# Local attention's scores as three fp32r products of query and key parts, with the rows of the low parts made on VectorE

## The reference, cut to what matters

```python
qkv = h @ wqkv                                  # h: the tokens, half of the channels shifted by one
q, k, v = split(qkv, 3)                         # 8 heads of 64
q, k = rotary_xpos(l2norm(q) * qs, l2norm(k) * ksc)
bq = q.reshape(b, h, w, 128, 64) * 8.0          # windows of 128 tokens
bk, bv = look_around(bk), look_around(bv)       # the window before and the own: 256 keys
sim = einsum("bhwid,bhwjd->bhwij", bq, bk)      # <- the change is here
sim = where(mask, -max, sim)
o = einsum("bhwij,bhwjd->bhwid", softmax(sim), bv)
x = x + o @ wo
```

## Time and profile before

| | |
|---|---|
| median of 3 runs | 1584.57 us (1582.27 to 1584.73) |
| the profiled execution, its own time | 1584.13 us |
| its span | 1582.3 us |
| mean granted TensorE clock | 0.985 |
| PE busy in the whole span | 1479.3 us, 93% |
| DVE, ACT, POOL busy | 1037.2, 894.0, 521.1 us |
| attention of the first layer | about 915 to 1135 us from the span's start |
| attention of the second layer | about 1254 to 1475 us |

### The profile page before, as it was taken

How to read it: one execution, slowest core, us unless ns; L and a number is a source line. 1 busy time by engine, 2 the same in 40 slices (tenths; PEclk the granted TensorE clock), 3 DMA queues, 4 the chain that set the end, 5 groups by cost and what they waited for, 6 DMA issues and landing times. The chain is left out here.

```text
span 1582.3 us, 24385 instructions
## 1 busy us (share of the span) xinstructions
PE 1479.3 (93%) x9004; PEld 964.7 (61%) x9004; DVE 1037.2 (66%) x1879; ACT 894.0 (56%) x1852; POOL 521.1 (33%) x317
## 2 busy tenths in 40 slices
PE   8889999999987899999998889999999889999998
PEld 3432222222225679797987557777777667777776
DVE  3768888888818646465566545566597666666685
ACT  5137777777771343434252268778543488778341
POOL 7100000000004300000004277977433478877222
PEclk9999999999999999999999999999999999999999
DMA  7730222200000312030304120000100100000010
GB/s 245 157 41 12 31 41 41 41 2 1 1 12 14 123 53 69 14 107 13 107 7 137 40 70 2 1 1 2 61 20 0 57 2 1 1 1 28 5 50 27
DMA packets 59476, 64.84 MB, mean 41 GB/s; under 512 B 15154, under 2 KB 48706, under 8 KB 59380
## 3 DMA queue, kind: packets, MB, share of 16 engines
q1 hardware_dynamic: 58020, 60.17, 14.7%
q10 hardware_dynamic: 1360, 3.41, 0.6%
HBM read 52.88 MB, written 10.49 MB: 40 GB/s over the span
## 5 line engine op out<-in xcount | busy, mean ns | idle before, releaser
L581 DVE TENSOR_REDUCE mcol<-bank 128x1 f32<-128x1024 f32 x256 | 302.1, 1217 | 56.7 <-PE bank L572 56.7
L669 ACT ACTIVATE a_pt<-bank 128x512 f32<-128x512 f32 x512 | 266.5, 604 | 89.1 <-PE bank L701 89.1
L701 PE MATMUL bank<-qa,ka 99*128 99x512 bf16 x512 | 193.7, 386 | 7.6 <-ACT a_pt L669 3.8
L572 PE MATMUL bank<-ka,qa 96*128 96x512 bf16 x512 | 192.7, 384 | 4.5 <-DVE mcol L581 1.4
L2040 DVE CUSTOM_DVE_ANT_0 w_sm<-bank,mask 128x256 f32<-128x256 f32 (+1 forms) x256 | 88.9, 404 | 119.6 <-PE bank L1624 119.6
L1583 PE MATMUL bank<-wqkv,w_hst 128*128 128x512 f32 x576 | 150.4, 405 | 5.6 <-DVE w_sinp L1980 5.2
L701 PEld LDWEIGHTS bank<-qa,ka 99*128 99x128 bf16 x512 | 49.1, 98 | 165.7 <-ACT a_pt L669 121.3
L712 PE MATMUL bank<-a_pt,vst 128*32 128x512 f32 x1024 | 136.4, 605 | 0.1
L1875 ACT ACTIVATE w_sm<-w_sm,w_st 128x256 f32<-128x256 f32 (+1 forms) x256 | 123.9, 488 | 19.9 <-DVE w_st L2040 19.7
L1483 POOL TENSOR_TENSOR w_sm<-w_sm,w_st 128x1024 f32<-128x1024 f32 (+1 forms) x64 | 116.7, 1823 | 25.7 <-DVE w_st L2047 25.6
L1583 PEld LDWEIGHTS bank<-wqkv,w_hst 128*128 128x128 f32 x576 | 104.2, 189 | 28.9 <-issue 8.1
(11 more groups left out here) (254 smaller groups left out, 2842.1 us busy)
## 6 DMA issues: line engine op xcount, KB each, us to landing
f_wex<-in_W SPq DMA_DIRECT2D x8, 2048.0 KB, 12.0
qa<-q_parts SPq DMA_DIRECT2D x48, 128.0 KB, 4.3
ka<-k_parts SPq DMA_DIRECT2D x48, 128.0 KB, 5.0
q_parts<-p_parts SPq DMA_DIRECT2D x16, 192.0 KB, 3.3
k_parts<-p_parts SPq DMA_DIRECT2D x8, 384.0 KB, 3.5
wqkv_raw<-in_wqkv SPq DMA_DIRECT2D x2, 1536.0 KB, 6.8
w_raw<-in_w SPq DMA_DIRECT2D x2, 1408.0 KB, 5.9
phi<-in_phi SPq DMA_DIRECT2D x5, 512.0 KB, 3.9
```

Source lines behind the costliest of these rows:

```text
L572: last = nc.tensor.matmul(max_bank(G, r)[:, jh * HALF:(jh + 1) * HALF], G["qa"][k][0:KS, hg % 2, h, it * P:(it + 1) * P], G["ka"][k][0:KS, ...
L581: nc.vector.reduce_max(G["mcol"][hg % 2][:, p:p + 1], max_bank(G, r)[:, :], X).then_inc(G["max_free"], 1)
L669: nc.scalar.activation(pt[n % 2][:, q, :], sbank(HG * step + q), ACT.Exp, scale=HD0 ** -0.5).then_inc(p_ready, 1)
L701: mm(sbank(i), ka[k][:, q, n * P:(n + 1) * P], qa[k][:, ih, q, :], start=True, stop=True).then_inc(st_ps, 1)
```

## The change

The queries and keys are kept in two fp32r tiles each, high and low. ACT's copies from PSUM now round into the high tiles. DVE gets a new step `low_rows`, two subtractions of 128x512 (PSUM minus the high tile), ahead of the first maxima of every slot. The scores are three fp32r matmuls for each head instead of one fp32 matmul, and PE waits for the low parts where it waited for ACT's copies. The queries have one buffer instead of two, so that their writers also wait for the scores of the window before. `split_tokens` moves, on DVE, from the start of the odd slots 3 to 13 to their end (6 times in a layer).

```diff
--- before.py
+++ after.py
@@ -1286,8 +1286,8 @@
             hst = own("w_hst", [P, 2, 2, KD, 2 * P], F32R)
             turned = own("w_turned", [P, 3, 2 * INNER])
             vsb = own("w_vsb", [P, VRING, INNER])
-            kT = own("w_kT", [P, HP, 2 * WIN])
-            qT = own("w_qT", [P, 2, HP, P])
+            qTs = [own(f"w_qT_{c}", [P, HP, P], F32R) for c in range(2)]
+            kTs = [own(f"w_kT_{c}", [P, HP, 2 * WIN], F32R) for c in range(2)]
             sm = own("w_sm", [P, 2, H1, 2 * WIN])
             PT = own("w_PT", [P, HP, 4, P])
             oT = own("w_oT", [P, 2, HP, P])
@@ -1329,6 +1329,7 @@
             "step", "on_ready", "t_ps", "x1_done", "rot_ps", "rot_out", "zeroed"))
         (h_high, h_low, qk_ps, v_ps, qk_sb, v_sb, sq_done, ss_done, n_square, n_sqrt, rn_done) = (sem("w_" + n) for n in (
             "h_high", "h_low", "qk_ps", "v_ps", "qk_sb", "v_sb", "sq_done", "ss_done", "n_square", "n_sqrt", "rn_done"))
+        q_low, k_low = sem("w_q_low"), sem("w_k_low")
         (cos_done, sin_done, add_done, turn_done, tq_ps, tk_ps, qT_done, kT_done, s_ps, s_masked, e_done,
          d_done, p_done, pt_ps, pt_act, pt_dve, pv_ps, oT_done, wo_ps, wo_done) = (sem("w_" + n) for n in (
             "cos_done", "sin_done", "add_done", "turn_done", "tq_ps", "tk_ps", "qT_done", "kT_done", "s_ps", "s_masked",
@@ -1356,6 +1357,9 @@
         def keys(i):
 
             return slice(0, 2 * WIN) if i % NW else slice(0, WIN)
+
+        def place_of(i):
+            return slice(i % 2 * WIN, (i % 2 + 1) * WIN)
 
         def mask_of(i):
             return mask[:, WIN * (1 - i % 2):][:, keys(i)]
@@ -1613,15 +1617,17 @@
 
                 def scores(l, i, half):
                     if half == 0:
-                        pe.wait_ge(qT_done, (NG * l + i) + 1)
-                        pe.wait_ge(kT_done, (NG * l + i) + 1)
+                        pe.wait_ge(q_low, (NG * l + i) + 1)
+                        pe.wait_ge(k_low, (NG * l + i) + 1)
                     pe.wait_ge(s_masked, H1 * (NG * l + i) + 4 * half)
                     n = keys(i).stop
                     for p in range(2 * half, 2 * half + 2):
-                        for e in range(2):
-                            c0 = (p % 2) * 2 * WIN
-                            rows = slice(HD1 * e, HD1 * e + HD1)
-                            last = mm(S_PS[e][:, c0:c0 + n], qT[rows, i % 2, p, :], kT[rows, p, 0:n], start=True, stop=True)
+                        c0 = (p % 2) * 2 * WIN
+                        for c, (cq, ck) in enumerate(PRODUCTS):
+                            for e in range(2):
+                                rows = slice(HD1 * e, HD1 * e + HD1)
+                                last = mm(S_PS[e][:, c0:c0 + n], qTs[cq][rows, p, :], kTs[ck][rows, p, 0:n],
+                                          start=(c == 0), stop=(c == len(PRODUCTS) - 1))
                     last.then_inc(s_ps, 1)
 
                 def hidden(u, f, part):
@@ -1853,11 +1859,12 @@
 
                     def query_rows(i):
                         act.wait_ge(tq_ps, before(i) + 1)
-                        S(qT[:, i % 2, :, :], four(T_PS[0]), ACT.Copy).then_inc(qT_done, 1)
+                        act.wait_ge(s_ps, 2 * before(i))
+                        S(qTs[0][:, :, :], four(T_PS[0]), ACT.Copy).then_inc(qT_done, 1)
 
                     def key_rows(i):
                         act.wait_ge(tk_ps, before(i) + 1)
-                        S(kT[:, :, (i % 2) * WIN:(i % 2 + 1) * WIN], four(T_PS[1]), ACT.Copy).then_inc(kT_done, 1)
+                        S(kTs[0][:, :, place_of(i)], four(T_PS[1]), ACT.Copy).then_inc(kT_done, 1)
 
                     def outputs(i):
                         act.wait_ge(pv_ps, before(i) + 1)
@@ -2041,6 +2048,14 @@
                                                    mask_of(i), -QK_SCALE, HIGHEST, ALU.add, ALU.min,
                                                    st[:, s, 1, h:h + 1]).then_inc(s_masked, 1)
 
+                    def low_rows(i):
+                        dve.wait_ge(qT_done, before(i) + 1)
+                        dve.wait_ge(s_ps, 2 * before(i))
+                        V.tensor_tensor(qTs[1][:, :, :], four(T_PS[0]), qTs[0][:, :, :].bitcast(F32), ALU.subtract).then_inc(q_low, 1)
+                        dve.wait_ge(kT_done, before(i) + 1)
+                        V.tensor_tensor(kTs[1][:, :, place_of(i)], four(T_PS[1]), kTs[0][:, :, place_of(i)].bitcast(F32),
+                                        ALU.subtract).then_inc(k_low, 1)
+
                     def inverse_sums(i, j):
                         hs = slice(4 * j, 4 * j + 4)
                         dve.wait_ge(e_done, 2 * before(i) + j + 1)
@@ -2058,10 +2073,10 @@
                         V.tensor_tensor(xs, four(O_PS)[:, 0:KD, :], xs, ALU.add).then_inc(wo_done, 1)
 
                     for t in SLOTS1[first:]:
-                        if t % 2 == 1 and t < NG - 1:
-                            split_tokens(l, (t + 1) // 2)
                         if there(t - 3):
                             inverse_sums(t - 3, 1)
+                        if there(t - 2):
+                            low_rows(t - 2)
                         if t == NG - 3:
                             centred(UNITS * l)
                         if t == NG - 2:
@@ -2086,6 +2101,8 @@
                         if there(t - 2):
                             inverse_sums(t - 2, 0)
                             maxima(t - 2, 1)
+                        if t % 2 == 1 and t < NG - 1:
+                            split_tokens(l, (t + 1) // 2)
                         if t == NG - 1:
                             for q in range(2):
                                 inverse(UNITS * l, q)
```

## The result

The changed kernel takes 1606.49 us (median of 4 runs, 1606.2 to 1608.32) against 1584.65 us: ratio 1.0149, 95% interval 1.0129 to 1.0169. It is slower by 21.8 us; the forecast was 16.4 (1601 us).

A forecast was written before the change was run, and what follows sets the result against it. PE was taken to bound the kernel. Per layer 6.0 + 3.2 - 1.4 - 0.9 gave +6.9; two layers 13.8, with the second's start 16.0, on 1584.1 us: 1601 us said, 8-in-10 range 1586 to 1620.

The forecast's parts named there:

- What bounds: First layer's attention: PE sets the pace, busy 194.0 of 210.0 us; DVE has spare time, but when its results come counts.
- The scores on PE: Four-head score call on PE: 12 fp32r matmuls in 6 side-by-side pairs save 0.15 us a call, near bounds 0 and 0.3.
- 12 matmuls one after the other: Rival for PE's score calls: a pair's heads take turns, 1.62 us a call, about 1660 us in all; chance 0.08.
- The calls with 128 keys: The 8 score calls on PE for windows with 128 keys: change taken at nothing.
- The low rows: DVE's two 0.69 us subtractions: hidden in slots with projections, uncovered in slots 3, 16 and 17, +3.2 us a layer.
- The moved split: End of odd slots: DVE's cast and subtraction wait for POOL, delaying L1587 (L1583 before): +1.0 us a slot pair, +6.0 a layer.
- rival (b): End of odd slots: the split loses two turns to POOL, L1583 is 3.3 us late, about 1627 us; chance 0.12.
- Slot 9: PE's 2.34 us gap there is partly paid back and the clock may not fall: -1.4 us a layer.
- The sum: Whole kernel: +6.9 us a layer, 13.8 for two layers, 16.0 with the second's start; 1601 us, 1.0% slower.
- with the second's start 16.0: Second layer's start: first scores wait for DVE's subtractions, so projections begin later, +2.2 us once, bringing the total to 16.0.

## Why the prediction was right, point by point

**What bounds.** Right: PE sets the pace in the slots; cheaper scores alone made the kernel 11.7 us faster, and the kernels with added PE waits were slower.

**The scores on PE.** Right: the two heads run together (12 matmuls one after the other were put at 1.62 us; the 12 took 0.98), and a call saves 0.16 (forecast 0.15). The calls with 128 keys, taken at nothing, cost 0.82 instead of 0.65 us to the next group, 1.3 us in all.

**The low rows.** Their duration was right (0.68 and 0.69 us), and POOL never held them up: all 64 took 0.65 to 0.69 us, 54 of them beside a running POOL instruction. Their view, min, median and max in ns:

```profile
L2054 DVE TENSOR_TENSOR w_qT<-bank,w_qT x32: 652/692/693, 917.8 to 1476.8; 128x512 fp32r<-128x512 f32 x32
```

In slot 3 the scores' wait grew from 0.54 to 1.39 us (forecast +0.7). Slot 16's wait grew from 1.84 to 3.37 and slot 17's from 0.79 to 1.62, which is +1.5 and +0.8, forecast 1.7 and 0.8.

**The moved split.** Right in mechanism, and near in size: in the first layer the pairs from slots 5, 7, 11 and 13 are 1.0, 1.1, 1.3 and 1.2 us longer (forecast 1.0), that from slot 3 1.4 (forecast 1.7 with its low rows), L1587 waiting 1.36 to 1.49 us. Who loses the turn was right too, but there was luck in it, since it hangs on tenths or hundredths: rival (b) was not a case of its own but a chance at each of the 12 places. No cast lost it in the changed kernel's trace; one did with the second layer's scores later, where nothing on that place was edited, and two in the second run of the split alone.

**Slot 9.** PE's gap fell from 2.34 to 1.42 us, and the transposes behind it took 1.06 us in both layers, so the clock had not fallen. Slot 9 alone is 2.65 and 2.82 us shorter; with slot 10, which has the split's wait, the pair is 0.9 and 1.0 us shorter, forecast 0.4.

```profile
1019.96 1.06 PE L1652 MATMUL bank<-ident,w_sm 128*128 128x128 f32 x8 [1.42 <-DVE w_PT L2068]
```

**The sum.** From the transposes of slot 2 to those of slot 2 of the next layer the first layer grew by 7.1 us, forecast 6.9. The second, to slot 17, grew by 15.6 us where the sum had 6.9 + 2.2. The step that was mis-sized is "with the second's start 16.0": I priced the wait (+2.2; PE's idle time was 2.09) and not the clock behind it. At the start the 18 projections took 2.4 us more than before and the scores 0.6 more than with this wait gone; in the second layer's slot 4 the new wait for the split came behind one of 1.38 for POOL, and L1587 ran at the low clock, 4.40 instead of 3.06; behind slot 16's wait of 3.37 the scores, the transposes and L1671 took 1.65, 1.97 and 2.86 instead of 0.97, 1.09 and 1.95. These come to 6.9 us, about the excess of 6.5:

```profile
1290.50 4.40 PE L1587 MATMUL bank<-wqkv,w_hst 128*128 128x512 f32 x12 [1.49 <-DVE w_hst L1977]
...
1465.69 1.65 PE L1629 MATMUL bank<-w_kT,w_qT 64*128 64x256 f32 x12 [3.37 <-DVE w_qT L2054]
1467.27 1.97 PE L1652 MATMUL bank<-ident,w_sm 128*128 128x128 f32 x8
1469.03 2.86 PE L1671 MATMUL bank<-w_oT,wo 128*128 128x128 f32 x16
```

When the clock falls is not settled by one wait: the same two waits, 1.38 for POOL and 1.49 for the split, stand in slot 12 of both layers, and there L1587 took 3.04 and 3.06 us.

What I had not foreseen at all is how much covers how much. The split's wait hid part of the low rows' price; with the split back, the low rows still cost 26 us. A part of that belongs to both: in slots 3 and 9 the split ahead of the low rows makes them late (PE waits 2.45 and 2.71 us). I did not separate the waits from the low clock by an experiment, and how the 26 us divide between them stays open.

## What to carry to other kernels

Before a VectorE cast, or a subtraction of two SBUF tiles, is moved to a place where TensorE will want it soon, look at what GpSimd runs there: each such instruction may cost the rest of GpSimd's running instruction, and two in a row cost two turns. Keep it away from work on VectorE that is urgent behind it, or let GpSimd wait for it: one wait on GpSimd took 10.7 us off here. Where a kernel's executions differ by such turns, read them in the trace before the time is put down to an edit. And price a new TensorE wait with the clock that may follow it: on top of one 2.1 us wait came 3.0 us of slower matmuls.

## What the runs showed of the hardware

Where VectorE's cast and GpSimd's probabilities are recorded within the same 0.01 us, the turn went either way: in one execution to GpSimd at 1024.01 and 1367.80 and to VectorE at 1310.19, in another of the same kernel to VectorE at 1024.10 and 1367.67. Executions of that kernel differed by 17.5 us. Only instructions of VectorE with all operands in SBUF were held up: the cast, the subtraction, and L1989 (1.99 us); those with a PSUM input were not. Nor were all of the first kind: in the changed kernel the sum L1993 took 1.20 to 1.22 us and the reciprocal L2001 0.34 to 0.35, beside GpSimd or not. The Trainium skill (SBUF — State Buffer, Who interferes with whom) calls it an exclusive lock for the whole instruction; the trace agrees, the subtraction ending 0.54 to 0.56 us behind GpSimd's instruction at all 12 places of the changed kernel. Two K = 64 fp32r matmuls of different row halves ran together, 12 of 256 columns in 0.98 us.
